# Expert rows added to the output in memory by GpSimd's accumulating scatters, one at a time, onto a residual stored early

## The reference

```
h = _L0_tok_ref(...)                                  # alignment, (32, 128, 128)
h = h + _L0_attn_ref(_layernorm(h), ...)              # attention, 8 heads
h = h + _L0_ffn_ref(_layernorm(h), ...)               # mixture of experts
# _L0_ffn_ref: for every row the two best of 8 experts, gates by softmax
topv, topi = top_k(x @ Wg, 2); w = softmax(topv)
y += gw[..., e] * (silu(x @ W[e]) * (x @ V[e])) @ W2[e]     # e = 0 .. 7, F = 512
```

## Time and profile before

| | |
|---|---|
| median of 3 runs | 887.12 us (887.08 to 888.9) |
| the profiled execution's own time | 885.96 us |
| its span | 884.1 us |
| first tile load issued | 629.3 us |
| first and last scatter start | 645.8 and 858.4 us |
| last instruction on an engine | 878.9 us |

### The profile page before, as it was taken

The page is one execution under the profiler, slowest core; times in us unless marked ns, Lnnn a source line. Parts: engine busy times, 40 slices in busy tenths (PEclk is TensorE's granted clock), DMA queues, the critical chain, the costliest instruction groups (busy, mean ns, idle before and its releaser), DMA issues.

```text
span 884.1 us, 13288 instructions
## 1 busy us (share of the span) xinstructions
PE 486.4 (55%) x2622; PEld 422.9 (48%) x2623; DVE 639.7 (72%) x2029; ACT 384.4 (43%) x956; POOL 294.8 (33%) x449
## 2 busy tenths in 40 slices
PE   2200000000001478889888998841399999999960
PEld 1100000000001366779778887841288888888850
DVE  3698989898946878698898776566166666676645
ACT  2254445454521355354544444210166666666640
POOL 1043444343410122132152563355223333333330
PEclk9999999999999999999999999999999999999985
DMA  4587211313034222112111100011111111111109
GB/s 93 114 164 129 49 37 41 54 25 65 13 75 142 73 74 57 49 62 81 49 46 40 51 22 9 21 38 50 49 40 44 42 42 45 42 41 47 42 13 283
DMA packets 113384, 54.17 MB, mean 61 GB/s; under 512 B 56652, under 2 KB 109132, under 8 KB 113251
## 3 DMA queue, kind: packets, MB, share of 16 engines
q1 hardware_dynamic: 106366, 44.60, 21.6%
q0 software_dynamic: 4352, 8.47, 2.9%
q10 hardware_dynamic: 2621, 0.62, 0.5%
HBM read 29.93 MB, written 24.26 MB: 61 GB/s over the span
## 4 chain that ended last, share of the span: by engine, by line
DVE 38%; PE 30%; issue 12%; DMA 7%; POOL 6%; ACT 3%; SPq 3%; ACTq 0%; DVEq 0%; POOLq 0%
DVE D L1177 8%; DVE D L1152 5%; PE ps L534 5%; PE ps L740 4%; POOL xd_dram L1036 4%; PE ps L536 4%; PE ps L535 4%; PE ps L720 4%; DMA xd_dram<-pay,slot 3%; ACT D L812 2%; DVE D L1143 2%; PE ps L620 2%; DVE rc L1321 2%; POOL sq L1027 2%; PE ps L739 2%
## 5 line engine op out<-in xcount | busy, mean ns | idle before, releaser
L625 PEld LDWEIGHTS ps<-va,pt 128*128 128x128 f32 x512 | 137.5, 351 | 0.0
L620 PE MATMUL ps<-eye_sb,sq 128*128 128x128 f32 x256 | 114.7, 454 | 28.4 <-DVE on L1337 27.9
L1027 POOL TENSOR_TENSOR sq<-sq,mn 128x1024 f32<-128x1024 f32 x32 | 67.2, 2099 | 189.3 <-ACT sq L884 185.1
L1063 POOL DMA_INDIRECT y_dram<-on,dest x72 | 70.7, 982 | 161.8 <-DVE on L1480 125.5
L570 PE MATMUL ps<-zdiag,ones_f 32*128 32x32 f32 x2 | 0.6, 406 | 219.2 <-DVE zdiag L1220 219.2
L625 PE MATMUL ps<-va,pt 128*128 128x17 f32 x512 | 114.7, 307 | 0.0
L620 PEld LDWEIGHTS ps<-eye_sb,sq 128*128 128x128 f32 x256 | 87.5, 343 | 48.9 <-issue 38.6
L1012 POOL TENSOR_TENSOR D<-D 128x128 f32<-128x128 f32 x130 | 56.2, 432 | 156.7 <-DVE D L1170 91.8
L570 PEld LDWEIGHTS ps<-zdiag,ones_f 32*128 32x128 f32 x2 | 0.5, 305 | 219.3 <-DVE zdiag L1220 219.3
L1451 DVE TENSOR_TENSOR sq<-sq,ps 128x512 f32<-128x512 f32 x72 | 49.5, 687 | 60.5 <-PE ps L536 44.1
L812 ACT ACTIVATE D<-D 64x2 f32<-64x2 f32 (+1 forms) x154 | 31.3, 203 | 111.3 <-DVE D L1152 90.5
(11 more groups left out here) (227 smaller groups left out, 1533.9 us busy)
## 6 DMA issues: line engine op xcount, KB each, us to landing
stage<-xd_dram SPq DMA_DIRECT2D x72, 65.0 KB
D<-th_dram SPq DMA_DIRECT2D x16, 208.0 KB, 4.5
g_dram<-D SPq DMA_DIRECT2D x14, 208.0 KB, 4.6
x_dram<-D SPq DMA_DIRECT2D x14, 208.0 KB, 4.7
h0q<-g_dram SPq DMA_DIRECT2D x8, 256.0 KB, 2.9
gb<-g_dram SPq DMA_DIRECT2D x8, 256.0 KB, 3.3
xf<-x_dram SPq DMA_DIRECT2D x8, 256.0 KB, 3.1
xb<-x_dram SPq DMA_DIRECT2D x8, 256.0 KB, 3.6
```

Source lines behind the costliest of these rows:

```text
L620: last = nc.tensor.transpose(ps[:, 5 + h // 4, T * (h % 4):T * (h % 4) + T], sq[n % 3][:, T * h:T * h + T], eye_sb[:])
L625: m = nc.tensor.matmul(ps[:, 7, (HD + 1) * h:(HD + 1) * (h + 1)], pt[turned % 2][:, T * h:T * h + T], va[q % 2][:, k, h, :], start=True, s ...
L1027: pool.tensor_tensor(v, v, bass.AP(tensor=m.tensor, offset=m.offset, ap=[m.ap[0], [1, NH], [0, T]]), ALU.subtract).then_inc(s_sub, 1)
L1063: pool.indirect_dma_start(y_dram, bass.IndirectOffsetOnAxis(dest[:, c:c + 1], 0), yrow[c], None, bounds_check=2 * NB * T - 1, oob_is_err=F ...
```

## The change

The intermediate tensor `y_dram` is gone. SP stores the residual of each group q to the output during attention (`store_base`, at offset -9, after `s_h1`). In the expert stage POOL's `add_rows` takes the place of `scatter`: the indirect DMA goes to the output itself with `compute_op=ALU.add`, so each row is added in memory to what stands there. Since two tiles can hold the same token, each scatter now waits for the landing of the one before it (`s_ys` of the previous slot). Both copies of a token carry the same destination number, 0 to 4095 (`tokid`), and the bounds check is at 4095. The first four scatters are written out ahead of the loop. SP's loads of `y_dram`, DVE's 16 adds and SP's 8 stores at the end are gone, and SP ends on the landings of the scatters.

```
-            pool.iota(tokid[:], [[NB * T, 2], [T, NB]], base=0, channel_multiplier=1).then_inc(s_consts, 1)
+            pool.iota(tokid[:], [[0, 2], [T, NB]], base=0, channel_multiplier=1).then_inc(s_consts, 1)
...
+            def store_base(q):
+                b = slice(4 * q, 4 * q + 4)
+                sp.wait_ge(s_h1, q + 1)
+                sp.dma_start(out[b].rearrange("b i j -> i b j"), h1[:, b, :]).then_inc(s_base, 16)
             for n in STEPS_OF_ATTENTION:
+                quad(store_base, n, -9)
...
-            for q in range(NQ):      # SP: y_dram loads (ya, yb), then the stores of h1
-                ...
+            pool.wait_ge(s_base, 16 * NQ)
-            def scatter(k, c):
+            def add_rows(k, c):
                 pool.wait_ge(s_dest, k + 1)
                 pool.wait_ge(s_y, k + 1)
+                if isinstance(k, int) and k > 0:
+                    pool.wait_ge(s_ys[(k - 1) % 4], 16 * ((k - 1) // 4 + 1))
+                elif not isinstance(k, int):
+                    pool.wait_ge(s_ys[(c + 3) % 4], round_of(k, c) if c else round_of(k, c) - 16)
                 pool.nop(nofuse=True)
-                pool.indirect_dma_start(y_dram, bass.IndirectOffsetOnAxis(dest[:, c:c + 1], 0), yrow[c], None,
-                                        bounds_check=2 * NB * T - 1, oob_is_err=False).then_inc(s_ys[c], 16)
+                pool.indirect_dma_start(out.rearrange("b t e -> (b t) e"),
+                                        bass.IndirectOffsetOnAxis(dest[:, c:c + 1], 0), yrow[c], None,
+                                        bounds_check=NB * T - 1, oob_is_err=False,
+                                        compute_op=ALU.add).then_inc(s_ys[c], 16)
...
-            for q in range(NQ):      # DVE: the two final adds of each group
-                b = slice(4 * q, 4 * q + 4)
-                dve.wait_ge(s_yl[q], 32)
-                V_.tensor_tensor(h1[:, b, :], h1[:, b, :], ya[q], ALU.add).then_inc(s_fin, 1)
-                dve.wait_ge(s_fin, 2 * q + 1)
-                V_.tensor_tensor(h1[:, b, :], h1[:, b, :], yb[q], ALU.add).then_inc(s_fin, 1)
```

More of the change, by code:

```diff
@@ L58, in tower @@
         xd_dram = nc.dram_tensor("xd_dram", (NX * REG + 128, ROW), f32).ap()
-        y_dram = nc.dram_tensor("y_dram", (2 * NB * T, E), f32).ap()
         fr, bf16 = mybir.dt.float32r, mybir.dt.bfloat16
@@ L218, in tower @@
         rowgate = sb("rowgate", [128, 4])
[L219 to L223, removed]
         s_in = sem("s_in")
@@ L253, in tower @@
         s_e2 = sem("s_e2")
-        s_out = sem("s_out")
+        s_base = sem("s_base")
         s_ohy = sem("s_ohy")
@@ L327, in tower @@
         s_ys = [sem(f"s_ys{k}") for k in range(4)]
-        s_yl = [sem(f"s_yl{q}") for q in range(NQ)]
-        s_fin = sem("s_fin")
         s_sc = [sem(f"s_sc{k}") for k in range(8)]
@@ L518, in _ @@
                 sp.wait_ge(s_ys[c], 16 * (TILES // 4))
-            for q in range(NQ):
-                b = slice(4 * q, 4 * q + 4)
-                y = y_dram.rearrange("(k b t) e -> k t b e", k=2, t=T)
-                sp.dma_start(ya[q], y[0][:, b, :]).then_inc(s_yl[q], 16)
-                sp.dma_start(yb[q], y[1][:, b, :]).then_inc(s_yl[q], 16)
-            for q in range(NQ):
[L525 to L528, removed]
         @block.tensor
@@ L1057, in _ @@
                 quad(send_others, n, -17)
-            def scatter(k, c):
+            pool.wait_ge(s_base, 16 * NQ)
+            def add_rows(k, c):
                 pool.wait_ge(s_dest, k + 1)
                 pool.wait_ge(s_y, k + 1)
+                if isinstance(k, int) and k > 0:
+                    pool.wait_ge(s_ys[(k - 1) % 4], 16 * ((k - 1) // 4 + 1))
+                elif not isinstance(k, int):
+                    pool.wait_ge(s_ys[(c + 3) % 4], round_of(k, c) if c else round_of(k, c) - 16)
                 pool.nop(nofuse=True)
-                pool.indirect_dma_start(y_dram, bass.IndirectOffsetOnAxis(dest[:, c:c + 1], 0), yrow[c], None,
-                                        bounds_check=2 * NB * T - 1, oob_is_err=False).then_inc(s_ys[c], 16)
-            with pool.Fori(0, TILES, 4) as t:
+                pool.indirect_dma_start(out.rearrange("b t e -> (b t) e"),
+                                        bass.IndirectOffsetOnAxis(dest[:, c:c + 1], 0), yrow[c], None,
+                                        bounds_check=NB * T - 1, oob_is_err=False,
+                                        compute_op=ALU.add).then_inc(s_ys[c], 16)
+            for k in range(4):
+                add_rows(k, k)
+            with pool.Fori(4, TILES, 4) as t:
                 for c in range(4):
-                    scatter(t + c, c)
+                    add_rows(t + c, c)
         @block.vector
```

## The result

The changed kernel takes 954.2 us (median of 4 runs, 952.1 to 954.87) against 887.98 (887.08 to 888.9): a ratio of 1.0742, with a 95% interval of 1.0719 to 1.0764. The forecast was 904.7 us with a range of 880 to 945: the right side, but 49.5 us short, so the predicted loss of 17 us is in truth 66. The profiled execution has a span of 953.0 us.

A forecast was written before the change was run, and what follows sets the result against it. The prediction took TensorE's 2.99 us a tile as the present bound and chained scatter landings as the new one. First scatter, 67 links of 3.11 + x, four empty links and last landing gave 871.2 + 67 x: 904.7 us, range 880 to 945.

The forecast's parts named there:

- The bound and the removed tail: Expert stage: TensorE sets a pace of 2.99 us a tile; the memory-traffic tail behind it, 23.5 us, leaves the path.
- The early stores at nothing: Attention: eight residual stores of 256 KB issued by SP cost 0, at worst 9 us.
- The link with plain writes: Expert stage, chained scatters: 0.81 us from landing to next start plus 2.3 us to landing, 3.11 us a link.
- first part: Each link of the scatter chain: from the semaphore to the start of the next DMA instruction, taken as 0.81 us.
- x: Each of 67 links: what adding in memory costs over a plain write, taken as 0.5 us within bounds 0 to 2.0.
- rival 2: Scatter chain: rows added nearly one by one, or far longer descriptor making; x 1.0 to 2.0, 938 to 1005 us; chance 0.15.
- The data-only rule: Adding scatters: the add costs only its second source read, so 0.19 us of data time comes again, sum 884.
- The empty slots: Last scatters, holding no rows: four links without x, at 0.81 + 2.1 us each.
- The end: After the last scatter's landing: 0.2 us to the end of the span, as the final stores have it.
- rival 3: Expert stage: TensorE's clock falls because it idles, up to 5.9 us a tile and 1071 us; chance 0.02.

## Why the prediction was right in its direction and wrong in its size

**The bound and the removed tail** were right. The 23.5 us are gone; the kernel with plain unchained scatters shows it as 19.5 us less than the kernel before, with the drain's part behind the last landing already in it (there its last scatter starts at 862.1 and its span ends at 869.9).

**The early stores at nothing** were right (ratio 1.0005). The first scatter of the changed kernel was 1.4 us later than that of the kernel before; half of that was there before the first store, and what it is stays open.

**The link with plain writes** was nearly right: 3.11 predicted, 3.22 measured. Its first part was 0.81 in the trace of before and is 0.93 in the mean of the chain, 8 us in all. Of these 3 us are the second wait in half of the links, shown by placing it differently; the rest is the first link of each round of the loop (0.94) and five links that took 1.0 to 1.7, whose cause stays open.

**The step that failed** is x, "I take 0.19 and a little over half of the 0.49, x = 0.5". It is 1.0 us. In 67 links the missing half comes to 34 us. Both of its parts were too small. For descriptors I had taken 0.3 us, out of 0 to 0.49, as a cost of each row; the instruction is 0.57 longer, and at least 0.27 of that doesn't depend on the number of rows. For data I had 0.19, a second pass of the same 16 packets, and it is some 0.4: the rows go one to a packet, and each DMA engine is busy 0.74 us instead of 0.19. Neither of the two was visible in a trace without an adding DMA; the bounds of 0 and 2.0 held it. What was wrong in the forecast was to take a value from the mechanisms that I could name as if none was left out, and to give x above 1.0 only 0.15.

So the run came out in rival 2's range, at its lower end of x = 1.0 (938 us, and 16 us from the other terms). That rival had two mechanisms. Its second, descriptors that take far longer to make, is half of what the runs show. Its first isn't shown as it was priced: eight reads one after another at 2.0 us each would be 16 us, and the whole landing takes 3.3. Whether an engine's eight rows overlap or follow each other at some 0.09 us each (0.74 / 8) stays open.

**The data-only rule**, which the Trainium skill (Collectives: The Full Stack, Why ReduceScatter is half of AllGather) gives, says that an add is slow for its second source read and not for the adding. Read as a rule on data alone, it doesn't hold here. In this kernel the bytes account for at most 0.4 of 1.0 us, by the estimate above. The measurement decides: for scatters of 128 rows of 512 bytes the data alone leaves out most of the cost.

**The empty slots** were put at 2.9 us each and took 3.6, and one 5.0: the four together cost 4 us more. An adding scatter with no row in bounds still pays for the longer instruction.

**The end** was put at 0.2 us behind the last landing and is 3.5. I had not looked at what each engine still does at the end. The row was in the trace of before.

**The clock** (rival 3) did fall a little, to a mean of 0.96 between 660 and 840 us. TensorE had 42 us of idle time there and the chain of waits goes from landing to landing, so it bounded nothing.

The terms together, in the profiled execution: 34 from x (one landing of 4.9 us in it), 8 from the first part, 4 from the empty slots, 1.4 from the start, 0.6 from the last landing and 3.3 from the drain are 51.3 us; the prediction's span was 901.6, the measured one 953.0, 51.4 apart.

## What to carry to other kernels

A DMA costs its duration when nobody waits for it and its whole time to landing when the next one does. Before chaining DMAs, multiply (wait to start + start to landing) by the number of links and compare it with the pace of the stage; here 4.2 us stood against 3.0, and what was a gain of 20 us without the chain turned into a loss of 66. Then ask which pairs can truly touch the same bytes: here only tiles of different experts, and waiting only where an expert begins made the same idea a gain of 1.4%.

If a cost has no row in the trace, take the sum of the mechanisms that you can name for a lower end and not for the middle; here it was half of the cost. And look at what an engine still does behind its last instruction: removing a tail can lay bare what it hid.

## What the runs showed of the hardware

- An indirect DMA of 128 rows of 512 bytes with `compute_op` add takes 1.55 us of GpSimd and lands in the memory after 3.3 us; the plain one takes 0.98 and 2.3. With 64 rows it is 1.40 us and 2.9; with rows of 256 bytes 1.55 and 3.1.
- It sends one packet for each row (144 packets in all, with 16 for the semaphore), the plain one 32.
- Unchained, 72 such DMAs, 3.0 us apart, cost the kernel nothing: 870.87 us against 871.15 with plain writes.
- From a landing to the start of the next indirect DMA on GpSimd pass 0.81 us, 0.90 if a second, long-met wait comes behind it, and 0.94 at the first scatter of each round of the loop.
- GpSimd's closing drain takes 6.1 us from the last adding scatter and 7.6 us from the last plain one, and so the span ends 3.5 and 5.6 us after the last landing. With adding scatters of 64 rows it takes 8.0 us, 5.7 beyond the last landing, so adding alone doesn't make it shorter. What it does in that time stays open.
